# Low one-hots of the places by ScalarE, one shared order of two PSUM banks, and expert sums in the tokens' old place

## The reference

```
h = QRNN(x)              # width-3 convolution to 3*128 gates, tanh/sigmoid, scan over time -> (64, 123, 128)
h = h + gelu(longconv(layernorm(h)) + h0 * layernorm(h))     # filter irfft(fft(B)/fft(1,A)) along time
h = h + moe(layernorm(h))
```

```
gate_logits = x @ gate_weight.T;  top_vals, top_idx = top_k(gate_logits, 2);  routing_w = softmax(top_vals)
h     = silu(einsum('td,efd->tef', x, w1))            # F = 512
h_sum = einsum('tef,te->ef', h, mask)                 # sum over the tokens of each expert
y_mean = einsum('ef,edf->ed', h_sum / counts, w2)
out   = sum_k routing_w[t,k] * y_mean[top_idx[t,k]]
```

## Time and profile before

| | |
|---|---|
| median of 3 executions | 491.23 us (489.1 to 493.98) |
| the profiled execution: time, span | 493.29 us, 491.5 us |
| PE / DVE / ACT / POOL busy | 82% / 64% / 45% / 45% of the span |
| granted TensorE clock, mean | 0.901 of full speed |
| end of the long convolution | 162.3 us |
| routing up to the token table | 162.3 to 238.9 us |
| first SiLU of the expert loop | 246.6 us |
| expert loop | to about 455 us |
| second layer and output | to 491.5 us |

### The profile page before, as it was taken

The page is one execution under the profiler, slowest core; times in us unless marked ns, Lnnn a source line. Parts: engine busy times, 40 slices in busy tenths (PEclk is TensorE's granted clock), DMA queues, the critical chain, the costliest instruction groups (busy, mean ns, idle before and its releaser), DMA issues.

```text
span 491.5 us, 7231 instructions
## 1 busy us (share of the span) xinstructions
PE 405.1 (82%) x1898; PEld 265.4 (54%) x1899; DVE 314.4 (64%) x800; ACT 221.5 (45%) x490; POOL 220.8 (45%) x236
## 2 busy tenths in 40 slices
PE   8999999997699895773768878787998888787882
PEld 7888888886699894552524323233333333233461
DVE  3598888888487999849725543534444454444893
ACT  3334554454233383750335555544555555455410
POOL 2011011102200499919665666666666666561700
PEclk9999999999799898776597998988878898898997
DMA  7206434321123833347011111111111111134038
GB/s 173 59 1 159 129 96 124 104 79 49 38 83 104 238 85 83 83 148 278 17 48 43 45 49 43 43 43 43 48 38 43 47 44 44 41 43 21 0 98 232
DMA packets 52076, 39.13 MB, mean 80 GB/s; under 512 B 20390, under 2 KB 45684, under 8 KB 52052
## 3 DMA queue, kind: packets, MB, share of 16 engines
q1 hardware_dynamic: 47492, 29.65, 21.6%
q0 software_dynamic: 4416, 9.05, 8.5%
q10 hardware_dynamic: 144, 0.13, 0.1%
HBM read 30.40 MB, written 8.42 MB: 79 GB/s over the span
## 4 chain that ended last, share of the span: by engine, by line
PE 50%; issue 29%; DVE 11%; POOL 3%; ACT 2%; another core or an unknown queue 2%; DMA 1%; POOLq 0%; ACTq 0%; DVEq 0%
PE P L807 30%; PE P L741 6%; PE P L794 5%; DVE arena L1324 3%; PE P L594 2%; DVE H L1482 2%; POOL rs L455 2%; PE P L846 1%; PE P L603 1%; ACT arena L1041 1%; PE P L586 1%; DVE arena L1402 1%; PE P L568 1%; DMA arena<-table,arena 1%
## 5 line engine op out<-in xcount | busy, mean ns | idle before, releaser
L807 PE MATMUL P<-w1T,arena 128*128 x276 | 162.6, 687 | 37.1 <-ACT arena L1041 27.0
L1441 DVE TENSOR_TENSOR BIG<-BIG,P 128x512 f32 x138 | 94.9, 688 | 116.6 <-ACT P L1045 56.8
L521 POOL DMA_INDIRECT arena<-table,arena x138 | 131.3, 952 | 78.1 <-issue 34.4
L1045 ACT ACTIVATE P<-P 128x512 f32<-128x512 f32 x138 | 80.7, 585 | 80.8 <-PE P L807 55.6
L807 PEld LDWEIGHTS P<-w1T,arena 128*128 128x128 f32 x276 | 46.6, 211 | 90.8 <-issue 90.4
L455 POOL TENSOR_TENSOR rs<-ve,mhalf 123x4 f32<-123x4 f32 x16 | 17.9, 1118 | 106.1 <-DVE ve L1097 106.1
L887 ACT ACTIVATE arena<-P 128x492 f32<-128x492 f32 x48 | 27.8, 582 | 50.4 <-PE P L550 50.4
L1041 ACT COPY arena<-P 128x128 f32<-128x128 f32 x138 | 37.4, 271 | 26.3 <-PE P L794 13.3
L794 PEld LDWEIGHTS P<-ident,arena 128*128 128x128 f32 x138 | 21.0, 152 | 49.4 <-issue 45.1
L794 PE MATMUL P<-ident,arena 128*128 128x128 f32 x138 | 40.6, 294 | 3.3 <-issue 3.2
L550 PE MATMUL P<-xh,wh 128*128 128x498 f32 x144 | 41.9, 399 | 0.0
(11 more groups left out here) (214 smaller groups left out, 584.3 us busy)
## 6 DMA issues: line engine op xcount, KB each, us to landing
arena<-kpad SPq DMA_DIRECT2D x16, 492.0 KB, 4.1
XN<-in_L_ffn_w SPq DMA_DIRECT2D x1, 4096.0 KB, 13.7
arena<-in_x SPq DMA_DIRECT2D x16, 224.0 KB
table<-XN SPq DMA_DIRECT2D x4, 896.0 KB
out<-H SPq DMA_DIRECT2D x8, 448.0 KB
arena<-table,arena POOLq DMA_INDIRECT x138
arena<-in_L_tok_kernel SPq DMA_DIRECT2D x3, 192.0 KB, 4.1
arena<-in_x SPq DMA_DIRECT2D x16, 26.0 KB
```

The source lines that it names most:

```text
L521: pool.indirect_dma_start(out=G[:, n % GBUF, :], out_offset=None, in_=table[:, :], in_offset=bass.IndirectOffsetOnAxis(ap=idx[:, n:n + 1], ...
L807: nc.tensor.matmul(P[k % 4][:, :], GT[:, k % 2], w1T[:, bass.ds(e * FF, FF)], start=True, stop=True).then_inc(expert_mm, 1)
L1045: nc.scalar.activation(P[k % 4][:, :], P[k % 4][:, :], ACT.Silu).then_inc(silu_done, 1)
L1441: v.tensor_tensor(at, at, P[k % 4][:, :], ALU.add).then_inc(esum_step, 1)
```

## The change

**One-hots.** VectorE makes 16 of the 32 columns, in two instructions of eight. ScalarE makes the other 16. For these, VectorE ANDs the rank with eight powers of two (`bits_i`), copies to float (`bits_f`), TensorE transposes (`bit_transposes`), ScalarE copies (`copy_bits`), TensorE multiplies with a constant matrix `matchb` (`matches`, four matmuls of 512 columns for a quarter), where an element is above 6 only for equal bits, and ScalarE applies ReLU with bias -6 (`low_onehots`). GpSimd makes none. A second buffer `ohl[1]` lies in `BIG`. **Banks.** The two banks `PR` are used by the transposes of h, of w1 and by the matches in one fixed order, counted by `ring_mm` and `ring_read`. **Norms.** GpSimd takes eight of 16 entries, ScalarE eight, VectorE none. **Order.** w1's m = 0 to 5 come before `picks(0)`, 6 to 9 after `pick_transposes(0)` and before `ranks(2)`, 10 to 15 after `count_all_mm`, just before the expert loop. **Sums.** `esum` is `XN`, cleared by two DMAs from the zero rows of `table`; `w2` goes to `BIG` after the last w1 transpose.

```diff
-NORM_DVE, NORM_POOL = 2, 5
+NORM_POOL = 8
-OB = 9
-ON_POOL = 5
+OB = 8
+OG = 4
+ON_ACT = 16
+PER_Q = ON_ACT // OG
+BITS = 8
-        esum = BIG[:, 0:E * FF]
+        w2_sb = BIG[:, 0:E * FF].rearrange("p (e f) -> p e f", e=E)
-        w2_sb = XN[:].rearrange("p b c -> p (b c)").rearrange("p (e f) -> p e f", e=E)
+        esum = XN[:].rearrange("p b c -> p (b c)")
+        W1_AT, MATCH_AT = {}, {}
+        at_ring = 2 * NHB
+        for part, q in ((range(0, 6), 0), (range(6, 10), 1), ((), 2), ((), 3), (range(10, E), None)):
+            for m in part:
+                W1_AT[m], at_ring = at_ring, at_ring + 1
+            for a in range(PER_Q if q is not None else 0):
+                MATCH_AT[q, a], at_ring = at_ring, at_ring + 1
# SP
+            sp.dma_start(match_in[:], match).then_inc(const_in, 16)
...
-                sp.wait_ge(xn2_ready, g + 1)
...
             sp.wait_ge(table_out, 2 * NQ * 16)
+            sp.wait_ge(zero_out, 32)
+            for h in range(2):
+                n = E * FF // 2
+                sp.dma_start(esum[:, h * n:(h + 1) * n],
+                             bass.AP(table.tensor, 0, [[0, 128], [1, n]])).then_inc(esum_zero, 16)
+            sp.wait_ge(ring_mm, W1_AT[E - 1] + 1)
             sp.dma_start(w2_sb, w2.rearrange("e d f -> d e f")).then_inc(w2_in, 16)
# GpSimd
+            nc.gpsimd.tensor_scalar(matchb[:], match_in[:], 1.0, None, ALU.mult).then_inc(match_ok, 1)
...
+            for i in range(7):
+                pool.memset(powers[:, i:i + 1], 2 ** i)
+            pool.memset(powers[:, 7:8], 2 ** 24).then_inc(pool_const, 1)
             norms(1)
             norms(2)
-            low_onehots(0)
             norms(3)
-            low_onehots(1)
-            for m in range(0, E // 2, 2):
-                clear(m)
-            low_onehots(2)
-            low_onehots(3)
-            for m in range(E // 2, E, 2):
-                clear(m)
# TensorE
+            def bit_transposes(q):
+                pe.wait_ge(bits_ready, q + 1)
+                if q >= 1:
+                    pe.wait_ge(bitsT_ready, q)
+                nc.tensor.transpose(PK[q % 2][:, 0:T], bits_f[0:T], ident[0:T, 0:T]).then_inc(bits_mm, 1)
+
+            def matches(q):
+                pe.wait_ge(bitsT_ready, q + 1)
+                for a in range(PER_Q):
+                    at = MATCH_AT[q, a]
+                    pe.wait_ge(ring_read, at - 1)
+                    rows = slice(a * OG * BITS, (a + 1) * OG * BITS)
+                    nc.tensor.matmul(PR[at % 2][0:T, :], bitsT[rows, :], matchb[rows, :],
+                                     start=True, stop=True).then_inc(ring_mm, 1)
...
-            for m in range(0, 4):
+            for m in range(0, 6):
                 w1_transposes(m)
+            pe.wait_ge(match_ok, 1)
+            bit_transposes(0)
+            matches(0)
             picks(0)
             pick_transposes(0)
+            for m in range(6, 10):
+                w1_transposes(m)
             ranks(2)
-            for m in range(4, 10):
-                w1_transposes(m)
+            bit_transposes(1)
+            matches(1)
             picks(1)
             pick_transposes(1)
-            for m in range(10, E):
-                w1_transposes(m)
             ranks(3)
...
-            picks(2)
+            bit_transposes(2)
+            matches(2)
             pe.wait_ge(tiles_ready, 1)
             nc.tensor.matmul(P[0][:, 10:11], befe[:], tilesb[:, 0:1], start=True, stop=True).then_inc(tile_base_mm, 1)
+            bit_transposes(3)
+            picks(2)
+            matches(3)
             pick_transposes(2)
             picks(3)
             pick_transposes(3)
...
             mm.then_inc(count_all_mm, 1)
-            pe.wait_ge(w1T_ready, E)
+            for m in range(10, E):
+                w1_transposes(m)
+            pe.wait_ge(ring_read, W1_AT[E - 1] + 1)
# ScalarE
+            def low_onehots(q):
+                for a in range(PER_Q):
+                    act.wait_ge(ring_mm, MATCH_AT[q, a] + 1)
+                    if q >= 2:
+                        act.wait_ge(pick_mm, 2 * QB * (q - 2) + (a + 1) * OG)
+                    nc.scalar.activation(ohl[q % 2][0:T, a * OG:(a + 1) * OG].rearrange("p n s -> p (n s)"),
+                                         PR[MATCH_AT[q, a] % 2][0:T, :], ACT.Relu,
+                                         bias=below[0:T]).then_inc(ring_read, 1)
...
-            for m in range(0, 4):
+            for m in range(0, 6):
                 copy_w1T(m)
             code_OH(1)
+            copy_bits(0)
+            low_onehots(0)
             copy_V(0)
+            for m in range(6, 10):
+                copy_w1T(m)
             for b in mine[2 * per:3 * per]:
                 norm2(b)
-            for m in range(4, 10):
-                copy_w1T(m)
             code_OH(2)
+            copy_bits(1)
+            low_onehots(1)
+            copy_V(1)
             for b in mine[3 * per:4 * per]:
                 norm2(b)
-            copy_V(1)
+            code_OH(3)
+            copy_bits(2)
+            low_onehots(2)
+            copy_bits(3)
+            copy_V(2)
+            low_onehots(3)
+            copy_V(3)
             for m in range(10, E):
                 copy_w1T(m)
-            code_OH(3)
-            copy_V(2)
-            copy_V(3)
# VectorE, in places(q)
-                v.tensor_copy(lob[0:T], loi[0:T])
-                if q >= 2:
-                    dve.wait_ge(onehot_pool, ON_POOL * (q - 1))
-                rs[0] += 1
-                v.tensor_copy(lof[0:T, q % 2], loi[0:T]).then_inc(route_step, 1)
+                v.tensor_copy(lob[0:T, q % 2], loi[0:T])
+                if q >= 1:
+                    dve.wait_ge(bits_mm, q)
+                step(v.tensor_tensor(bits_i[0:T], picked[0:T, 0:ON_ACT].bitcast(I32).unsqueeze(2).to_broadcast([T, ON_ACT, BITS]),
+                                     powers[0:T].unsqueeze(1).to_broadcast([T, ON_ACT, BITS]), ALU.bitwise_and))
+                v.tensor_copy(bits_f[0:T], bits_i[0:T].rearrange("p n i -> p (n i)")).then_inc(bits_ready, 1)
...
-            for part in range(ON_DVE // OB):
+            places(3)
+            for part in range(2):
                 low_onehots(2, part)
+            for part in range(2):
+                low_onehots(3, part)
             placed(1)
-            places(3)
...
-            for part in range(ON_DVE // OB):
-                low_onehots(3, part)
...
-            dve.wait_ge(esum_clear, E // 2)
+            dve.wait_ge(esum_zero, 32)
```

More of the change, by code:

```diff
@@ L67, with match_table @@
 ARENA = 10128
+def match_table():
+    s = np.arange(128)
+    rows = [(2.0 * (s >> i & 1) - 1) / 2 ** i for i in range(7)]
+    rows.append(sum(1.0 - (s >> i & 1) for i in range(7)) / 2 ** 24)
+    t = np.zeros((128, OG, 128))
+    for r in range(128):
+        t[r, r // BITS % OG] = rows[r % BITS]
+    return t.reshape(128, OG * 128)
 def tables():
@@ L85, in tables, with build @@
             2.0 ** (8 * np.arange(NCHUNK)[None, :] + np.arange(128)[:, None] // E - EXPO)], 1),
+        "match": match_table(),
     }
     return {k: v.astype(np.float32) for k, v in out.items()}
-def build(nc, x, wconv, fa, fb, h0, gate, w1, w2, dft, idft, route, out, kpad, table):
+def build(nc, x, wconv, fa, fb, h0, gate, w1, w2, dft, idft, route, match, out, kpad, table):
     ctx = ExitStack()
@@ L159, in build @@
         loi = carve(2 * QB, dt=I32)
-        lof = carve(2, 2 * QB)
-        lob = carve(2 * QB, dt=BF16)
-        ohl = carve(2 * QB, 128, dt=BF16)
+        bits_i = carve(ON_ACT, BITS, dt=I32)
+        bits_f = carve(ON_ACT * BITS)
+        bitsT = carve(T, dt=BF16)
+        powers = carve(BITS, dt=I32)
+        lob = carve(2, 2 * QB, dt=BF16)
+        ohl = [carve(2 * QB, 128, dt=BF16)]
         OHc = carve(2, 2 * QW, dt=BF16)
@@ L221, in build @@
         h0c = sb("h0c", [128, 1])
+        below = sb("below", [128, 1])
         gateT = sb("gateT", [128, WARM])
@@ L310, in build @@
         onehot = sem("onehot")
-        onehot_pool = sem("onehot_pool")
+        bits_ready = sem("bits_ready")
+        ring_read = sem("ring_read")
+        ring_mm = sem("ring_mm")
+        bits_mm = sem("bits_mm")
+        bitsT_ready = sem("bitsT_ready")
+        match_ok = sem("match_ok")
+        esum_zero = sem("esum_zero")
         code_mm = sem("code_mm")
@@ L475, in _ @@
             pool.memset(biasb[:], BIAS)
+            pool.memset(below[:], -6.0)
             nc.gpsimd.tensor_scalar(rankb[:], rank_in, 1.0, None, ALU.mult).then_inc(pool_const, 1)
@@ L902, in copy_w1T @@
                 e = (m + E // 2) % E
-                act.wait_ge(w1_transposed, m + 1)
+                act.wait_ge(ring_mm, W1_AT[m] + 1)
                 if m == 0:
                     act.wait_ge(zero_out, 32)
-                nc.scalar.copy(w1T[:, e * FF:(e + 1) * FF], PR[m % 2][:, :]).then_inc(w1T_ready, 1)
+                    act.wait_ge(match_ok, 1)
```

(28 more changed lines are left out.)

69 lines of the change are left out of this document (27 added, 42 removed).

## The result

The changed kernel takes 503.92 us (median of 4 runs, 499.02 to 505.15); the kernel before took 490.53 us beside it (4 runs, 489.1 to 493.98). The ratio is 1.0247 [1.0185, 1.0308]: **2.5% slower**. The forecast was 487.7 us, too near the time before to be told from it, with a range of 481.5 to 494.5; the result lies outside. The profiled execution has a span of 502.9 us and a time of 504.66 us.

A forecast was written before the change was run, and what follows sets the result against it. VectorE was taken as the bound from 221 to 245 us. Earlier first SiLU -3.8, buffered gathers -0.5 and sharing with w2's load +0.8 summed to -3.5 us: 491.2 becomes 487.7 us, range 481.5 to 494.5.

The forecast's parts named there:

- (a): Norms, quarter 1: GpSimd's extra tiles delay the second root, so VectorE waits 1.3 us.
- (c): Quarter 0's one-hots on ScalarE and TensorE: its picks end near 198.2 us, 0.6 us later than before.
- (d): Third count: w1 transposes ahead of it delay its read from 200.65 to 204.3 us, with VectorE idle 6 us.
- (e): Fourth count: read at 216.0 us instead of 218.99, 3.0 us earlier, with nearly no VectorE idle ahead.
- (f): VectorE from fourth count to token numbers: 11.8 us instead of 17.2, 2.5 us of it from one-hots without memsets beside them.
- C: Point where the token numbers are ready: forecast at 231.2 us instead of 238.9, 7.7 us earlier.
- (g): Tail from token numbers to loop: last 24 w1 transposes now exposed, so first SiLU comes only 3.8 us earlier, at 242.8.
- (h): DMA: clearing the sums done at 235.3 us, before the first sum; w2 beside the loop's start costs 0.8 us.
- R: Weights VectorE finishes after ScalarE's sigmoids, in the tail; forecast ready at 242.8 us and releasing the first SiLU.
- rival R3: Clearing DMA is late, ending at 256 us, so the first sum waits 13 us: 497 us; chance 0.08.
- rival R1: Faster TensorE clock lets the routing gain arrive: first SiLU near 239, -7.5 us, 483.7 us; chance 0.28.

The follow-up runs named there:

- kernel 10: Same program as kernel 1 (changed kernel, expert table padded to a multiple of 16 bytes), rerun on another chip: 483.61 us, ratio 0.9853.
- kernel 7: Changed kernel with aligned expert table, sums cleared by GpSimd memsets instead of DMA: 453.54 us, ratio 0.9851.
- kernel 11: Changed kernel with aligned expert table, earlier sigmoids, shorter warming, and first register load ahead of the last 24 w1 transposes: 482.17 us, ratio 0.9822.
- kernel 4: kernel 1 with w2 loaded only after 48 expert tiles: 456.39 us, ratio 0.99.
- Kernel 2: Kernel before the change with only the expert table moved two words, to 8 bytes past a multiple of 16: 474.59 us, ratio 1.0316.
- kernel 3: Changed kernel, table still misaligned, with thirty tiny matmuls moving the loop's code 60 instructions on: 473.77 us, ratio 1.0286.
- kernel 1: Changed kernel with the expert table padded two words to start at a multiple of 16 bytes: 454.68 us, ratio 0.9894.

## Why the prediction was wrong

**The step that failed** is a sentence in the first part: "The expert loop and what follows are the same instructions in both kernels, so I work out only when the first SiLU comes". The instructions are the same, their operands' addresses are not. One load of 12 registers in front of each round became 2 us longer, and TensorE, which bounds the loop, cannot hide it. Its clock falls more as well: the mean granted clock from 262 us to 430 us is 0.86 in the changed kernel and 0.91 in kernel 10. 1.8 us by ten rounds and 2.1 us for the first load are 20 us; by ratios the misaligned table costs 1.0247 - 0.9853 = 3.9% of 491 us, 19 us, in the changed kernel and 3.2% of 460 us, 14.5 us, in the kernel before. The prediction had named the observation that would refute it, the loop changing by more than 2 us, but no rival and no chance went with it: the loop's own instructions were put at nothing, and the range held only what the routing, the tail and the transfers left uncertain.

Point by point, by the trace of the changed kernel less its shift of 1.8 us, or by kernel 10, whose convolution ends where that of before does (162.44 and 162.32):

(a) A wait of 1.3 us for the second root: 0.49 us, so the place was right and the size too large. (c), (d) DVE idle of 5 to 7 us at the third count and a read at 204.3: 6.34 us and 206.07 - 1.8 = 204.3, right. (e) The fourth count at 216.0: 217.79 - 1.8, and 216.07 in kernel 10, right; nearly no idle time was named, 1.47 us was seen.

(f) C 7.7 us earlier: L1477 at 233.00 - 1.8 = 231.2, as forecast, and all eight one-hots 0.25 us each. Kernel 7 does not measure the 2.5 us credited to the missing memsets: in the kernel before the four memsets ran back to back and held VectorE up as a whole, in kernel 7 the two take turns, and C comes 0.6 us later.

(g) The order was right: 24 transposes (4.97 us, forecast 5.16), then load and warming. Two sizes were off: load and last copy, put at 1.4 us, took 3.84 us misaligned and 1.75 us aligned, and the warming, put at 2.4 us, took 4.90 us, all at the lower level, and 4.24 in kernel 10, two thirds of its records at the lower level: in kernel 10 the last 8 transposes are already faster (0.15 us each) than the 16 before them (0.22), but behind the gap the clock is down again. It need not be: kernel 7 has the same gap and warms in 2.69 us, near the forecast. So TensorE, and not R, releases the first SiLU. In kernel 10 it comes 2.6 us earlier than before (244.04), where 3.8 had been forecast: two thirds of (f), not half, are given back, and kernel 11 recovers 2.5 us of them.

(h) The clearing's two parts were issued from 223.45 on (SP's queue in order of time, the DMA issues with their median, and the times to landing of L451 in the changed kernel):

```profile
223.45 1.01 SPq L451 DMA_DIRECT2D XN<-table  x2
...
238.02 0.38 SPq L454 DMA_DIRECT2D BIG<-in_L_ffn_w  x1
```
```profile
XN<-table SPq DMA_DIRECT2D x2, 2048.0 KB, 9.6
```

```profile
DMA to landing us min/median/max: 7.4/9.6/11.8
```

9.6 is the middle of 7.4 and 11.8; the second part, issued 0.4 us behind the first, landed last, 12.2 us after the first issue, at 235.65 - 1.8 = 233.9. The 13.7 us taken from w2 gave 235.3: right within 1.5 us. That is well ahead of the first sum, which waited for ScalarE: rival R3 is refuted. w2 beside the loop costs nothing that kernel 4 could show.

The sum of the costed steps, -3.5 us or a ratio of 0.993, has its test in kernel 10: 0.9853 [0.9819, 0.9887], -7.2 us, and 0.9894 [0.985, 0.9939] on the other chip, -4.9 us. The sign is right, the size is small by 1 to 4 us. The first SiLU explains 2.6 us, less than forecast. The rest lies in the loop, and where it comes from stays open. In the two profiled executions the loop takes 209.5 us (before) and 200.9 us (kernel 10), but not by a steady gain: from SiLU to SiLU the first twelve tiles take 22.3 and 16.3 us, the next twelve 17.5 and 20.4. Both stand ahead of expert products all along, 37.1 and 33.2 us in all; the stand of 4.40 us for "remote" is one of these. Kernel 2's trace has only 0.6 us of them, but the other traces of its group have 0.6 to 0.8 us too, so it does not tell whether the change removed any.

-7.2 us is also the size of rival R1, -7.5 us, but not by its path: R1 wanted C near 229.7 and the first SiLU near 239, and kernel 10 has 231.15 and 244.04. That agreement is luck.

## What to carry to other kernels

When a change resizes buffers, list what moved, and above all where tables lie from which an engine loads registers inside a loop: keep them at a multiple of 16 bytes (shown here for TensorE's loads of twelve). "The same instructions" is an argument only if their addresses are the same too; two words of padding were here worth more than the whole change. An idle time put down to "issue" at a fixed place of every round was here the engine's own register load, so read the code for register work there.

## What the runs showed of the hardware

- A load of 12 registers by TensorE from its on-chip table showed as 0.84 us of idle time from a multiple of 16 bytes and as 2.86 us from 8 past one, in the same kernel. 8 and 12 past pay alike. In the first two groups of runs, where the loop has no other stands, such a stand of 2.5 us is followed in most rounds by a fall of the granted clock to half (kernel 3: 0.51 from 279.5 to 283 us). VectorE's part is not seen: with TensorE's table alone misaligned the ratio is 1.0298 [1.0271, 1.0324], with both 1.0319 [1.0297, 1.0341]; VectorE's alone was not tried. By the Trainium skill, Runtime: NRT & Kernel Launch, Instruction fetch mechanics, a register load (from HBM) takes some 0.2 us a register; the idle time here, from the on-chip table, comes to 0.24 us a register misaligned and 0.07 us aligned, if all of it is the load.
- One program differs in time from chip to chip, and the difference lies in the loop. Kernels 1 and 10 are the same program and take 454.7 and 483.6 us. The first SiLU comes at 243.68 and 244.04, the end behind the loop takes 35 us in both, the loop 172.4 and 200.9 us. Busy time of each engine and granted clock from 262 us to 416 us, kernel 10 and then kernel 1 (columns as in the earlier trace rows):

```profile
262.00:416.00 154.00, 123.46 (x310) 49.47 (x309) 70.72 (x103) 79.49 (x207) 97.12 (x104) 0.91 0.17 44
```
```profile
262.00:416.00 154.00, 141.85 (x361) 52.44 (x359) 84.01 (x123) 94.71 (x243) 109.61 (x116) 1.00 0.23 50
```

Most of it is idle time of TensorE ahead of its expert products, 33.2 us in kernel 10 against the 0.6 us of kernel 1 shown under experiment 3:

```profile
L851 PE MATMUL P<-w1T,arena 128*128 x276 | 158.0, 670 | 33.2 <-ACT arena L1107 21.5 <-issue 11.4
```

The clock is not the whole of it: the stands that end at 264.39 (1.83 us) and 311.27 (2.76 us) have no fall of the clock beside them. What makes the engines stand on that chip is not shown. In kernel 1 the rounds are 15.0 us each, all alike, and paced by the gathers; in kernel 10 they vary between 16.6 and 18.7 us.
- 4 MB in two parts of 2 MB, all partitions reading the same 16 KB of DRAM each, landed 7.4 and 11.8 us after their issues, 12.2 us in all: no slower than a load of 4 MB of different data (13.7 us).
